# Token rows scattered to expert slots: no token lists, combination by gathers, another order of the edge work

## The reference

```python
xn  = layernorm(x)                                     # (6250, 256)
agg = segment_sum(edge_weight[:, None] * xn[col], row) # 200000 edges
q, k, v = xn @ Wq, xn @ Wk, xn @ Wv
mix = q @ batchnorm(softmax(k, over nodes).T @ v)
h   = x + agg + mix
hn  = layernorm(h)
p   = softmax(hn @ router_w.T)                         # 8 experts, the best 2, weights divided by their sum
for e in range(8):
    y = gelu(hn @ w1[e] + b1[e]) @ w2[e] + b2[e]
    out = out + combine[:, e:e+1] * y                  # out starts as h + hn
```

## Time and profile before

| | us |
|---|---|
| median of three executions | 2375.08 (2373.32 to 2385.05) |
| the profiled execution | 2391.07 |
| its span, from the first to the last instruction | 2389.3 |
| TensorE busy | 2092.6 (88%) |
| DVE busy | 1496.7 (63%) |
| GpSimd busy | 1420.8 (59%) |
| ACT busy | 1148.2 (48%) |
| mean granted TensorE clock | 0.949 of full |

### The profile page before, as it was taken

How to read it: one execution, slowest core, us unless ns; L and a number is a source line. 1 busy time by engine, 2 the same in 40 slices (tenths; PEclk the granted TensorE clock), 3 DMA queues, 4 the chain that set the end, 5 groups by cost and what they waited for, 6 DMA issues and landing times. The chain is left out here.

```text
span 2389.3 us, 36271 instructions
## 1 busy us (share of the span) xinstructions
PE 2092.6 (88%) x11864; PEld 1786.0 (75%) x11864; DVE 1496.7 (63%) x2726; ACT 1148.2 (48%) x3466; POOL 1420.8 (59%) x1282
## 2 busy tenths in 40 slices
PE   5798589998999899989998999899999964888885
PEld 3476477987888789878987888789889963666664
DVE  7895387758775777587758775877467766010112
ACT  4520154555456545554565455545566640333332
POOL 1001667667776776677667776776666621666663
PEclk9998899999999999999999999999999986999996
DMA  7523722232233222322232223222233321555666
GB/s 248 164 71 120 246 89 80 84 92 81 77 87 93 79 79 84 91 82 80 84 91 80 80 87 91 78 83 83 86 112 116 116 86 43 180 182 183 209 210 226
DMA packets 157570, 270.85 MB, mean 113 GB/s; under 512 B 28310, under 2 KB 105125, under 8 KB 157385
## 3 DMA queue, kind: packets, MB, share of 16 engines
q0 software_dynamic: 59584, 161.78, 22.7%
q1 hardware_dynamic: 62796, 72.81, 9.3%
q10 hardware_dynamic: 35004, 33.93, 4.8%
HBM read 223.61 MB, written 45.77 MB: 113 GB/s over the span
## 5 line engine op out<-in xcount | busy, mean ns | idle before, releaser
L1154 POOL DMA_INDIRECT edge_G<-xn_scratch,edge_row_i x1029 | 1165.7, 1133 | 488.2 <-issue 262.2
L1254 ACT ACTIVATE edge_weighted<-edge_hots,bins_scale 128x128 f32<-128x128 bf16 x2401 | 738.7, 391 | 52.3 <-DVE edge_row_hots L1311 52.3
L1221 PE MATMUL edge_op<-edge_win,edge_A 128*128 128x256 f32 x2744 | 663.6, 385 | 60.5 <-issue 43.4
L1221 PEld LDWEIGHTS edge_op<-edge_win,edge_A 128*128 128x128 f32 x2744 | 523.7, 192 | 148.6 <-issue 55.3
L1245 ACT COPY edge_A<-edge_ap 128x512 f32<-128x512 f32 x343 | 200.8, 585 | 734.9 <-PE edge_ap L1204 530.2
L1217 PE MATMUL edge_op<-edge_G,edge_weighted 128*128 128x256 f32 x2058 | 511.0, 384 | 25.8 <-DVE all_xn L1324 21.4
L1306 DVE TENSOR_TENSOR edge_hots<-bins_iota128b,bins_recb 128x1024 bf16<-128x1024 bf16 x343 | 237.1, 691 | 367.8 <-PE edge_ap L1204 272.0
L1217 PEld LDWEIGHTS edge_op<-edge_G,edge_weighted 128*128 128x128 f32 x2058 | 364.7, 191 | 71.8 <-DVE all_xn L1324 25.6
L1204 PEld LDWEIGHTS edge_ap<-edge_weighted,edge_row_hots 128*128 128x128 f32 x2744 | 359.1, 194 | 54.0 <-DMA edge_win<-xn_scratch 13.6
L1204 PE MATMUL edge_ap<-edge_weighted,edge_row_hots 128*128 128x128 f32 x2744 | 371.5, 279 | 15.8 <-DMA edge_win<-xn_scratch 13.2
L1311 DVE TENSOR_TENSOR edge_row_hots<-all_iota,bins_recd 128x512 f32<-128x512 f32 x343 | 238.5, 695 | 0.0
(11 more groups left out here) (291 smaller groups left out, 1849.3 us busy)
## 6 DMA issues: line engine op xcount, KB each, us to landing
exp_w1x<-in_w ACTq DMA_DIRECT2D x105, 256.0 KB
edge_G<-xn_scratch,edge_row_i POOLq DMA_INDIRECT x1029
exp_ys<-ys_scratch SPq DMA_DIRECT2D x12, 1024.0 KB
ln_xin<-in_x SPq DMA_DIRECT2D x12, 512.0 KB, 5.7
xn_scratch<-ln_xnb ACTq DMA_DIRECT2D x12, 512.0 KB, 6.8
xnT_scratch<-ln_xT SPq DMA_DIRECT2D x12, 512.0 KB, 7.0
mix_xg<-xn_scratch SPq DMA_DIRECT2D x12, 512.0 KB, 3.9
mix_ek<-xnT_scratch SPq DMA_DIRECT2D x12, 512.0 KB, 4.8
```

Source lines behind the costliest of these rows:

```text
L1154: pool.indirect_dma_start(out=G[:, t % AHEAD, i, :], out_offset=None, in_=xn_dram, in_offset=bass.IndirectOffsetOnAxis(ap=row_i[:, q % 2, ...
L1221: last = nc.tensor.matmul(op[j][:, :], A[:, j, i, :], win[:, q % 2 * DN + i, :], start=False, stop=i == DN - 1)
L1254: last = nc.scalar.activation(weighted[:, t % 2, i, :], hots[:, t % 2, i // 2, :, i % 2], ACT.Copy, scale=scale[:, b, i:i + 1])
```

## The change

- The bins' plan: LINKS_A_STEP is 4, the start of the slots has a step of its own (START_AT), and all later steps of the plan move back by two. The records of a batch have two copies (`q % 2`), so that `dve_decode` moves to step 47 of the batch and the one-hots and the `finish` of the batch's seam stand in the loop. There are three banks for `edge_op` and one for `edge_ap`. The windows of batch 0 are loaded in the mix stage; the 13 stores of `sum_scratch` are spaced by finished steps; the flag's chain moves to step 8 of the last batch.
- Two scratch tables: `xs_scratch` (13440 rows of 256, a slot for each row of each expert tile) and `ys_scratch` of the same shape. ACT's queue clears xs in the mix stage (21 transfers of 655 KB), and SP copies it into ys in the edge stage (21 transfers of 655 KB from memory to memory, at steps 6+8i of batches 1 to 5).
- The list block is gone. The route block works out `where` (the tile) and `place` (the slot) of each node and choice, SP loads all of hn (`ffn_hn`, 13 loads, 6.4 MB) ahead of w2s, and all of w1 (2 MB) later.
- GpSimd scatters the rows of hn to their slots in xs (98 indirect DMAs, SCB=4 in flight), then gathers the results of each group of nodes from ys (98 indirect DMAs) and stores `out`. SP loads a tile of 128 slots as a plain block as soon as `sent` reaches the number of scatters that it needs, and stores results as plain blocks. ACT copies the expert's w1 out of the resident table instead of loading it.

```diff
-    LINKS_A_STEP = 5
+    LINKS_A_STEP = 4
...
-    SLOT_AT = BASE_AT + 1
+    START_AT = BASE_AT + 1
+    SLOT_AT = START_AT + 1
...
+                def clear(n):
+                    rows = slice(n * ZT * P, min((n + 1) * ZT, NXT) * P)
+                    sp.dma_start(ys_dram[rows, :], xs_dram[rows, :]).then_inc(xs_zero, 16)
...
                 for q in range(2, NQ):
                     sp.wait_ge(stepped, (q - 1) * NB)
                     load_windows(q)
+                    for i in range(CLEARS):
+                        if (q - 2) * CLEARS + i < ZERO_DMAS:
+                            sp.wait_ge(stepped, (q - 1) * NB + 6 + 8 * i)
+                            clear((q - 2) * CLEARS + i)
...
                 sp.dma_start(b2e[:, :], b2).then_inc(wx_in, 16)
+                for g, rows in enumerate(ROWS):
+                    dst = hn[:, g * GT:(g + 1) * GT, :] if g < NG else hn[0:TAIL, g * GT, :]
+                    sp.dma_start(dst, node_view(hn_dram, g, rows)).then_inc(hn_in, 16)
                 sp.dma_start(w2s[:, :, :, :], w2.rearrange("e (c p) f -> p e c f", p=P)).then_inc(wx_in, 16)
...
+                for i in range(NXT + STORE_LAG):
+                    if i < NXT:
+                        tokens = sp.value_load(need_i[0:1, i:i + 1], min_val=2, max_val=NS)
+                        wait_then_pass(sp, sent, tokens, passed)
+                        if i >= XB:
+                            sp.wait_ge(t1_done, i - XB + 1)
+                        sp.dma_start(xt[:, i % XB, :], xs_dram[i * P:(i + 1) * P, :]).then_inc(x_in[i % XB], 16)
+                    t = i - STORE_LAG
+                    if t >= 0:
+                        sp.wait_ge(y_done, t + 1)
+                        sp.dma_start(ys_dram[t * P:(t + 1) * P, :], yt[:, t % YB, :]).then_inc(y_out[t % YB], 16)
...
+                for n in range(NS):
+                    t, k = divmod(n, 2)
+                    r = rows_of(t)
+                    if n >= SCB:
+                        pool.wait_ge(scattered[n % SCB], 16 * (n // SCB))
+                        pool.sem_inc(sent, 1)
+                    pool.indirect_dma_start(
+                        out=xs_dram, out_offset=bass.IndirectOffsetOnAxis(ap=place[0:r, k, t:t + 1], axis=0),
+                        in_=hn[0:r, t, :], in_offset=None, bounds_check=NXT * P - 1, oob_is_err=False)\
+                        .then_inc(scattered[n % SCB], 16)
...
+                    for s in range(len(rows)):
+                        for k in range(2):
+                            pool.indirect_dma_start(
+                                out=ys[0:r, j, s, k * D:(k + 1) * D], out_offset=None, in_=ys_dram,
+                                in_offset=bass.IndirectOffsetOnAxis(ap=place[0:r, k, g * GT + s:g * GT + s + 1], axis=0))\
+                                .then_inc(ys_in[j], 16)
...
-                    act.dma_start(w1x[:, t % XB, :, :],
-                                  w1[bass.ds(number_of[t], 1), :, :].rearrange("a (c p) f -> p (a c) f", p=P))\
-                        .then_inc(w1_in[t % XB], 16)
+                    nc.scalar.copy(w1x[:, t % WB, :, :].rearrange("p c f -> p (c f)"),
+                                   w1s[:, bass.ds(number_of[t], 1), :, :].rearrange("p a c f -> p (a c f)"))\
+                        .then_inc(w1_put, 1)
```

More of the change, by code:

```diff
@@ L1081, in edge_stage @@
         scores = bins.base[1][:, 0:NT * NEXP].rearrange("p (t e) -> p t e", e=NEXP)
-        win_in = [st.sem(f"win_in{j}") for j in range(2)]
+        win_in = bins.win_in
         h_saved = [st.sem(f"h_saved{j}") for j in range(4)]
@@ L1923, in expert_block @@
-def expert_block(nc, hn_dram, ys_dram, w1, b1T, w2s, b2p, wx_in, bias_in, token, target, expert, share, number, iota128, h,
-                 out, ident):
-    AHEAD = 7
+                link(v.tensor_reduce(pos[:, :, :], mine[:, :, :, :], AX.X, ALU.add))
+                link(v.tensor_copy(turn_i[:, :, :], pos[:, :, :]))
+                link(v.tensor_single_scalar(turn_i[:, :, :], turn_i[:, :, :], 7, op=ALU.arith_shift_right))
+                link(v.tensor_copy(turn[:, :, :], turn_i[:, :, :]))
@@ new lines, in _ @@
+                link(v.tensor_tensor(mine[:, :, :, :], under[:, :, :, :], both_over_e(turn), ALU.add))
+                link(v.tensor_tensor(mine[:, :, :, :], mine[:, :, :, :], both_over_t(tiles), ALU.min))
+                v.scalar_tensor_tensor(line[:, :, :], turn[:, :, :], -float(P), pos[:, :, :], ALU.mult, ALU.add)
+                link(v.tensor_reduce(where[:, :, :], mine[:, :, :, :], AX.X, ALU.add))
+                link(v.scalar_tensor_tensor(place[:, :, :], where[:, :, :], float(P), line[:, :, :], ALU.mult, ALU.add))
@@ new lines, in _ @@
+                link(v.tensor_reduce(own[:, :], gw[:, :], AX.X, ALU.add))
+                link(v.scalar_tensor_tensor(own[:, :], number[:, 0:1], float(NEXP), own[:, :], ALU.mult, ALU.add))
+                link(v.tensor_scalar(part[:, :], ident[:, 0:NXT], own[:, 0:1], None, ALU.mult))
+                assert n[0] == KEYED, n
+                dve.wait_ge(pe_c, 2)
+                link(v.tensor_scalar(part[:, :], keyed[:, :], own[:, 0:1], None, ALU.is_lt))
+                link(v.tensor_reduce(at[:, :], part[:, :], AX.X, ALU.add))
@@ L1928, in expert_block @@
+                link(v.tensor_scalar(put[:, :], iota128[:, 0:NXT], at[:, 0:1], own_e[:, 0:1], ALU.is_equal, ALU.mult))
+                assert n[0] == PLACED, n
+                dve.wait_ge(pe_c, 3)
+                link(v.tensor_copy(expert[:, :], owned[:, :]))
+def expert_block(nc, hn, hn_in, xs_dram, xs_zero, ys_dram, w1s, b1T, w2s, b2p, wx_in, bias_in, where, place, expert, share,
+                 number, iota128, h, out, ident):
     DOWN = 3
-    XB = 4
+    XB = 6
+    WB = 4
     YB = 4
-    CBUF = 4
+    CBUF = 3
+    SCB = 4
+    STORE_LAG = XB + 4
@@ L2139, in _ @@
+                link(v.tensor_tensor(late[:, :], where[:, 0, :], where[:, 1, :], ALU.max))
+                link(v.memset(last_f[:, :], 0.0))
+                assert n[0] == ENDS
                 dve.wait_ge(pe_c, 1)
-                link(v.tensor_reduce(least[0:NXT, :], dn[0][0:NXT, 0:P], AX.X, ALU.min))
-                link(v.tensor_scalar(holds[0:NXT, :], until[0:NXT, :], least[0:NXT, 0:1], number1[0:NXT, 0:1],
-                                     ALU.is_gt, ALU.mult))
+                v.tensor_reduce(latest[0:NT, :], dn[0][0:NT, P:2 * P], AX.X, ALU.max)
@@ L2148, in _ @@
[L2148 to L2154 removed]
+                link(v.tensor_reduce(need[0:NXT, :], dn[1][0:NXT, 0:NT], AX.X, ALU.max))
@@ L2157, in _ @@
                     j, r = g % CBUF, rows[0]
-                    dve.wait_ge(ys_in[j], 16 * (g // CBUF + 1))
+                    dve.wait_ge(ys_in[j], 16 * 2 * sum(len(ROWS[i]) for i in range(j, g + 1, CBUF)))
                     if g >= CBUF:
```

486 lines of the change are left out of this document (213 added, 273 removed).

## The result

The changed kernel takes 2476.57 us (median of 4, 2473.12 to 2481.6) against 2375.1 for the kernel before: the ratio is 1.043, 95% interval 1.041 to 1.045. It is slower by 101 us. The forecast was 2304 with a range to 2372.

What follows compares the result with a forecast made beforehand. TensorE bounds the edge stage; in the expert stage neither TensorE nor GpSimd is full. Edge -37 and expert stage with list block -34 take 2391 to 2320, as profiled; median forecast 2304 us, range 2235 to 2372.

Steps and rivals of the forecast that it cites:

- until tile 43 at +135 the scatters set the pace: Expert stage: tiles wait for GpSimd's 98 scatters, 3.1 us a tile until tile 43; 61 tiles follow at TensorE's pace.
- the pace of 2.38: Expert stage: TensorE's time per tile in us if the 2.45 us holds go; 2.7 was taken, 3.3 if they stay.
- the stage's start: Expert stage: starts at 2005 instead of 2017 (list block -32, later route block +20), without the edge's gain.
- the holds stay and follow GpSimd: Rival: TensorE's idle times come where GpSimd issues back to back and stay; pace 3.3, +23, total 2361; chance 0.15.
- The edge stage: Edge stage terms summed: -12 - 15 - 3 - 8 - 1 + 2 = -37 us.
- The seam: Edge stage, between batches: decoding leaves it, 5.90 us becomes 3.99, six seams, -12 us.
- The idle time of 14.6 us in the third step: Start of the edge stage: thirteen sum stores run beside gathers while ACT idles; spacing them gives -8 us.
- the slot steps: Edge stage: these steps, set by DVE, were to keep their 5.1 us; TensorE-bound steps take 3.99.
- three `edge_op` banks: Edge stage: the third bank priced at nothing, as TensorE waits for its own step's copy in any case.
- The route block: Before the expert stage: 6.4 MB of hn loads ahead of w2s delay `route_b2q`, +20 us (17 to 27).
- The scatters: Start of the expert stage: GpSimd's 98 scatters at 1.33 us each, 130 us in all.
- The clears: Edge stage: 21 clears at 0.1 us each, +2; rival that they collide with gathers, 2354, chance 0.12.

Runs made afterwards that it cites:

- p1: The kernel before with GpSimd's edge gathers paced, at most two in flight: 2571.68 us, where the kernel before takes 2243.
- e1: The new edge plan with the expert part of the kernel before, without the clears: 2241 and 2244 us against 2240 and 2237 before.

## Why the prediction was wrong

**The step that failed** is in the expert stage: "until tile 43 at +135 the scatters set the pace". On the chip of the result ten tiles had started by then, and the next one started at +143. Rows would have been there: on the second chip, with the same code, 42 tiles start, and TensorE ends 286 us after the stage's first scatter, where the same sum gives 287 at the pace of 2.38. What is missing from the sum is TensorE's slowness beside indirect DMAs in an unbroken row. Behind the last scatter stand 95 tiles in place of 61: 34 x 2.38 = 81 us. And these take 290 us, where 2.38 each and three tiles of lag would be 233: 57 us of pauses, where I had put 20 (2.7 less 2.38, 61 times). Together that is 118; TensorE ends at +425 in place of +310, 115 later. The rest of the miss is the stage's start, 40 us later than forecast (nearly all of it the edge stage's 37, below), and the end, 47 us in place of 40. The three add up to the 162 us between the profiled execution and the 2320 forecast for one like it.

The rival "the holds stay and follow GpSimd" named the circumstance, and I had its evidence in the earlier trace rows. Its price was wrong: I took the pace of before, 3.3 us a tile, as the worst. But that was the pace of a GpSimd that waits for tiles between its DMAs; with 98 in a row and 8 us of waits among them, ten tiles started in 135 us. (The sum was off too: at 3.3 it gives 135 + 201 + 10 + 40 = +386, not +407, so the rival's own time was 2340, not 2361.) The kernel before had kept GpSimd's queue tied to TensorE's progress, and the change untied it. The slowness doesn't set in with the first DMA of a row: in the scatters TensorE's updates come late after some 16 to 18 of them, in the group of eight that I looked at after 4 or 5.

**The edge stage: -37 forecast, nothing measured.** Most of the single terms came. The seam (rows of the changed kernel at the end of batch 2, TensorE, to be held against the earlier trace rows):

```profile
998.99 1.16 PE L1239 MATMUL edge_ap<-edge_weighted,edge_row_hots 128*128 128x128 f32 x8
...
1003.01 1.05 PE L1239 MATMUL edge_ap<-edge_weighted,edge_row_hots 128*128 128x128 f32 x8
...
1006.93 1.05 PE L1239 MATMUL edge_ap<-edge_weighted,edge_row_hots 128*128 128x128 f32 x8
```

4.02 and 3.92 us in place of 5.90. The idle time of 14.6 us in the third step is gone too; in steps 0 to 4 of the first batch ACT idles less than 6. And more than I had forecast: the slot steps, which I left at 5.1 us, are 3.91 apart. Before, TensorE waited in them for DVE's `finish`:

```profile
815.35 1.56 PE L1217 MATMUL edge_op<-edge_G,edge_weighted 128*128 128x256 f32 x6 [1.66 <-DVE all_xn L1324]
```

With three `edge_op` banks it no longer does, a part that I priced at nothing. I looked at the wait for the copy of the step and not at the one for `summed` right behind it.

All of it is given back. Batches 1 to 5 take 237 to 243 us as before. This is GpSimd and TensorE in batch 4, in the steps 16 to 22, right behind the short ones:

```profile
1319.26 3.56 POOL L1189 DMA_INDIRECT edge_G<-xn_scratch,edge_row_i  x1 [0.30 <-issue]
...
1323.13 2.81 POOL L1189 DMA_INDIRECT edge_G<-xn_scratch,edge_row_i  x1 [0.30 <-issue]
...
1328.19 1.53 PE L1252 MATMUL edge_op<-edge_G,edge_weighted 128*128 128x256 f32 x6 [0.74 <-DMA edge_G<-xn_scratch,edge_row_i]
...
1335.01 1.53 PE L1252 MATMUL edge_op<-edge_G,edge_weighted 128*128 128x256 f32 x6 [1.78 <-DMA edge_G<-xn_scratch,edge_row_i]
...
1359.31 0.59 ACT L1280 COPY edge_A<-edge_ap 128x512 f32<-128x512 f32 x1 [10.72 <-remote]
```

A gather takes 2.8 and 3.6 us there in place of 0.95, while DVE works through the bins' two-input instructions (of the 42 gathers over 2 us in this trace, 24 stand beside the large additions of the slot steps and 12 beside the one-hot matrices of the slots that follow). With slot steps of 5.1 us GpSimd kept a lead of 7 us or more (from the end of its last issue for a step to TensorE's use of it); with 3.9 it falls to 2.3, and TensorE waits for gathers. GpSimd, which has to catch up, then issues 20 gathers in an unbroken row, from 1330.11 on, until ACT idles 10.72 us for a late TensorE. That the catching up causes this last part is my reading; p1, which was to test it, didn't run on the first chip. On the second chip there is little of the last part, and the plan alone still gains nothing, as GpSimd's gathers set the steps 16 to 19 there too (up to 12 us for one).
The Trainium skill (GPSIMD Engine Reference, Specifications) says that GpSimd's port to on-chip memory is shared with VectorE, with contention for DVE instructions with two such inputs; the 3.56 us beside `TENSOR_TENSOR` instructions with two inputs agree.

**What was right.** The route block: `route_b2q` 29.75 us after the block starts in place of 9.3, so 20.4 later, forecast 20.

```profile
1957.68 14.26 SPq L1766 DMA_DIRECT2D ffn_hn<-hn_scratch  x13
...
1987.04 0.40 ACT L1756 CAST route_b2q<-ffn_b2e 8x256 bf16<-8x256 f32 x1 [27.42 <-DMA ffn_b1T<-in_b]
```

The scatters: 995 ns and 0.30 of issue, 1.29 us, where the scatter of before gave 1.33; with 8 us of waits for landings 135 us in all, forecast 130. The clears cost nothing that can be seen. The list block is gone.

**What stays open.** Why a row of indirect DMAs slows TensorE's instructions to 0.53 us, whether a long row of plain ones would, and why on one chip and not on the other, no run tells. It doesn't come with the change: the kernel before has it too, and its expert part takes 55 us longer on the first chip (446.5 us from the last `edge_A` copy to the end, 391.3 in e1's kernel on the second), the changed one's 135 (535.4 and 400.8).

## What to carry to other kernels

An idle time whose releaser is "remote" is a price to be explained before a change that makes more of what runs beside it: here those that the forecast had to price lay in unbroken rows of indirect DMAs, and the change made a row of 98. When an engine's queue is untied from the consumer, ask what its waits had been good for besides order; a bound on what is in flight (two in place of four) cost 42 us of scatters on the first chip and gave 65 back, while on the second it only cost. And when a step gets shorter, look at whose lead it lives on: TensorE's shorter steps ate GpSimd's. A verdict from one chip may be the chip's: this one is 4% on the first and nothing on the second.

## What the runs showed of the hardware that I had not expected

- Beside indirect DMAs that GpSimd issues every 1.26 to 1.29 us in a row, TensorE's semaphores come 4.2 to 4.3 us apart for four matmuls with their loads, and 2.1 for two (0.53 us an instruction), on one chip; on another 0.45 us for four, or 0.86 at half clock. With rows of at most two indirect DMAs, or beside plain DMAs of GpSimd at 255 GB/s in rows of up to eight, it isn't seen.
- The same kernel takes 2375 us on one chip and 2240 on another, and the verdict on a change follows: 1.04 on one, 1.003 on the other. The changed kernel's profiled executions show where: the last 24 steps of batch 1 take 111.8 us on the first chip and 111.1 on the second, but its steps 0 to 24, in which the holds lie, 127.6 and 114.1, and the expert part 535.4 and 400.8.
- The granted clock is at its lower level from 1951 on, when TensorE's work of the edge stage ends, and on the first chip stays there for most of the scatters (0.55 over their 139 us, in which TensorE's records are busy for 35), while on the second it is 0.94 from 1926 to 2036, with TensorE busy for 101 of 110 us. The low clock alone doesn't make the slowness: it gives 0.86 us for four matmuls, not 4.2.
- A gather of 128 rows by GpSimd takes up to 3.56 us beside DVE's two-input instructions, 0.95 otherwise.
